# Softmax rounds issued two ahead in a four-layer cross-attention kernel

## What is computed

```python
# layers 0, 3 (latent), H=512, 16 heads of 32
h = jnp.concatenate([x, latents], axis=1)
q = (latents @ q_w + q_b).reshape(b, k_len, NH, DH)
kv = (h @ kv_w + kv_b).reshape(b, p + k_len, NH, DH, 2)
attn = jnp.einsum('bkhd,bnhd->bhkn', q, kmat) / DH
attn = jnp.where(full_mask[:, None, None, :], attn, -jnp.inf)
attn = jax.nn.softmax(attn.astype(jnp.float32), axis=-1).astype(q.dtype)
attn_out = jnp.einsum('bhkn,bnhd->bkhd', attn, v).reshape(b, k_len, H)
attn_out = attn_out @ out_w + out_b + residual
out = rmsnorm(attn_out, postnorm_w)
out = jax.nn.gelu(out @ mlp_w1 + mlp_b1) @ mlp_w2 + mlp_b2
return out + residual
# layer 1 (grouped): 32 query heads on 8 key heads of 16, softmax, Wo, residual, layer norm
# layer 2 (cross): layer norm, q, k, v, 16 heads of 32, softmax, cproj, residual, layer norm, MLP, residual
```

## Time and profile before

| | us |
|---|---|
| median of 3 runs (2697.95 to 2700.19) | 2698.76 |
| the profiled execution | 2698.54 |
| its span | 2696.8 |
| PE busy (92% of the span) | 2478.5 |
| DVE / POOL / ACT busy | 1284.3 / 1104.4 / 1090.2 |

### The profile page before, as it was taken

How to read it: one execution, slowest core, us unless ns; L and a number is a source line. 1 busy time by engine, 2 the same in 40 slices (tenths; PEclk the granted TensorE clock), 3 DMA queues, 4 the chain that set the end, 5 groups by cost and what they waited for, 6 DMA issues and landing times.

```text
span 2696.8 us, 47930 instructions
## 1 busy us (share of the span) xinstructions
PE 2478.5 (92%) x18464; PEld 2080.7 (77%) x18464; DVE 1284.3 (48%) x2527; ACT 1090.2 (40%) x3705; POOL 1104.4 (41%) x1972
## 2 busy tenths in 40 slices
PE   7999998999997777758888899999899999899999
PEld 6887886888886666647777788888788888688887
DVE  4556554323226878764445533322355555432322
ACT  4555553111117777755555411111355555311111
POOL 2444446400135888973454570003345444540000
PEclk9999999999998999879989899999999999899999
DMA  4112213111122222221232241101211211321100
GB/s 154 56 56 89 70 36 106 62 45 47 59 74 70 78 91 77 66 69 61 84 103 89 73 125 48 47 34 61 83 48 48 87 48 34 105 63 47 48 32 16
DMA packets 110321, 181.25 MB, mean 67 GB/s; under 512 B 7889, under 2 KB 43409, under 8 KB 109073
## 3 DMA queue, kind: packets, MB, share of 16 engines
q1 hardware_dynamic: 110096, 178.19, 20.2%
HBM read 132.02 MB, written 46.14 MB: 66 GB/s over the span
## 4 chain that ended last, share of the span: by engine, by line
PE 78%; DVE 8%; ACT 5%; POOL 5%; issue 3%; DMA 1%; SPq 0%; DVEq 0%; POOLq 0%; ACTq 0%
PE banks L317 70%; PE banks L453 4%; ACT plain_high L697 3%; PE banks L480 3%; POOL plain_high L1268 2%; DVE neg_max L948 2%; DVE plain_high L944 2%; PE banks L504 1%; DVE plain_work L953 1%; DVE rounded_work L1046 1%; DVE rounded_work L1020 0%; DVE stats L1072 0%; DMA plain_work<-mlp_w 0%; POOL rounded_high L308 0%; PE banks L442 0%
## 5 line engine op out<-in xcount | busy, mean ns | idle before, releaser
L317 PE MATMUL banks<-rounded_work,rounded_low 128*128 128x512 f32 (+1 forms) x2688 | 533.1, 356 | 57.9 <-issue 35.3
L1268 POOL TENSOR_SCALAR plain_high<-plain_high,inv_sum 128x128 f32<-128x128 f32 (+1 forms) x1024 | 388.1, 402 | 407.7 <-DVE inv_sum L966 407.2
L317 PEld LDWEIGHTS banks<-rounded_work,rounded_low 128*128 128x128 f32 x2688 | 445.7, 200 | 124.7 <-issue 53.8
L317 PE MATMUL banks<-rounded_work,rounded_high 128*128 128x512 f32 (+1 forms) x2400 | 488.2, 358 | 8.7 <-DMA rounded_work<-ctx_split 6.2
L925 ACT ACTIVATE plain_work<-banks,columns 128x512 f32<-128x512 f32 x192 | 132.5, 690 | 865.3 <-PE banks L317 865.3
L317 PEld LDWEIGHTS banks<-rounded_work,rounded_high 128*128 128x128 f32 x2400 | 399.7, 193 | 76.4 <-issue 9.8
L1244 DVE CAST rounded_work<-plain_work 128x512 fp32r<-128x512 f32 x192 | 101.3, 528 | 693.7 <-ACT plain_work L925 682.8
L317 PE MATMUL banks<-rounded_low,rounded_work 128*128 128x512 f32 x1728 | 413.1, 391 | 0.0
L317 PE MATMUL banks<-rounded_high,rounded_work 128*128 128x512 f32 (+1 forms) x1728 | 392.8, 380 | 0.0
L317 PEld LDWEIGHTS banks<-rounded_low,rounded_work 128*128 128x128 f32 x1728 | 322.3, 188 | 68.8 <-issue 3.0
L317 PEld LDWEIGHTS banks<-rounded_high,rounded_work 128*128 128x128 f32 x1728 | 311.8, 190 | 60.4 <-issue 1.4
(11 more groups left out here) (101 smaller groups left out, 3063.4 us busy)
## 6 DMA issues: line engine op xcount, KB each, us to landing
plain_work<-x SPq DMA_DIRECT2D x96, 256.0 KB, 2.9
plain_work<-mlp_w SPq DMA_DIRECT2D x96, 256.0 KB, 2.7
rounded_work<-ctx_split SPq DMA_DIRECT2D x24, 1024.0 KB, 6.0
u<-plain_work SPq DMA_DIRECT2D x48, 256.0 KB, 2.8
plain_work<-u SPq DMA_DIRECT2D x12, 1024.0 KB, 6.7
x<-plain_work SPq DMA_DIRECT2D x48, 256.0 KB, 2.1
plain_work<-attention_w SPq DMA_DIRECT2D x44, 256.0 KB, 2.7
plain_work<-inputs_t SPq DMA_DIRECT2D x8, 1024.0 KB, 8.1
```

What stands on the lines that cost most here:

```text
L317: mm = pe.matmul(dst, lhs(i), rhs(j), start=first and n == 0, stop=last and n == 2, skip_group_check=True)
L1268: last = pool.tensor_scalar(part, part, inv_sum[:, R % 2, r, g:g + 1], 1.0, ALU.mult, ALU.mult)
```

## The change

In every layer a quarter now begins with turning the probabilities of its own round R and then issues the scores of round R + 2; before, it issued the scores of R + 1 first and then turned R. ACT copies both of its turned banks before the exponentials, DVE both of its own before the maxima, and the two inverses of a round are placed one by one, the second behind `dve_heads`. In the cross layer the keys and queries are projected two couples ahead (`pe_cross_pair`), the values one couple ahead, and the first input of the cross layer is turned and split within the last couple of the grouped layer; its DMAs are issued there too. The core of the diff:

```diff
@@ pe_gqa
             for p in range(PAIRS):
                 more = p + 1 < PAIRS
-                pe_scores(pe, y, p, 1)
                 pe_turn_probs(pe, y, p, 0)
+                pe_scores(pe, y, p, 2)
...
-                pe_scores(pe, y, p, 2)
                 pe_turn_probs(pe, y, p, 1)
+                pe_scores(pe, y, p, 3)
...
                 pe_turn_probs(pe, y, p, 3)
+                if more:
+                    pe_scores(pe, y, p + 1, 1)
+                    pe_queries(pe, y, p + 1, 1)
+                pe_attend(pe, y, p, 3)
+                if not more:
+                    pe_turn_x(pe, L[2], 0)
                 pe_out(pe, y, 2 * p)
-                pe_attend(pe, y, p, 3)
@@ pe_cross
+            pe_scores(pe, y, 0, 1)
+            pe_turn_x(pe, y, 1)
+            pe_cross_pair(pe, y, 1)
             for p in range(PAIRS):
...
                 pe_turn_probs(pe, y, p, 0)
                 if more:
-                    pe_turn_x(pe, y, p + 1)
+                    pe_scores(pe, y, p + 1, 0)
+                    pe_values(pe, y, p + 1, 0)
+                if p:
+                    pe_out(pe, y, 2 * p - 1)
                 pe_attend(pe, y, p, 0)
...
+                pe_turn_probs(pe, y, p, 1)
+                if more:
+                    pe_scores(pe, y, p + 1, 1)
+                if far:
+                    pe_turn_x(pe, y, p + 2)
...
                 pe_out(pe, y, 2 * p)
                 pe_attend(pe, y, p, 1)
-                if more:
-                    for i in range(2):
-                        pe_values(pe, y, p + 1, i)
+                if far:
+                    pe_cross_pair(pe, y, p + 2)
@@ act_round
             if turned:
                 act_probs(act, y, *turned, 0)
+                act_probs(act, y, *turned, 2)
             if k is not None:
                 act_exp(act, y, p, k, 0)
-            if turned:
-                act_probs(act, y, *turned, 2)
-            if k is not None:
                 act_exp(act, y, p, k, 1)
             between()
@@ dve_gqa
-                dve_round(dve, y, p, 2, (p, 1), nothing)
+                dve_invert(dve, y, p, 2, 1)
+                dve_round(dve, y, p, 3, (p, 1))
+                dve_invert(dve, y, p, 3, 0)
                 if p:
                     dve_again(dve, y, 2 * p - 1)
                 if more:
                     dve_queries(dve, y, p + 1, 0)
                 dve_heads(dve, y, p, 1)
@@ sp_gqa, last couple
+                else:
+                    wait_filled(sp, v_last(y, p))
+                    sp_c(sp, L[2], 0)
+                    sp_x(sp, L[2], 0)
+                    sp_mask(sp, L[2], 0)
```

346 lines of the change are left out of this document (190 added, 156 removed).

## The result

The changed kernel takes 2735.66 us (median of 4 runs, 2734.2 to 2739.52) against 2698.36 (2692.72 to 2700.19): ratio 1.0146, 95% interval 1.0132 to 1.0159. It is slower by some 37 us, where 12 less were forecast, and outside the range of 2654 to 2718 us. The profiled execution's span is 2737.7 us, 40.9 more than before.

The account below looks back on a forecast made before the run. PE was taken to fill the latent layers and MLPs, a chain across engines to pace the grouped layer. +15 - 20.5 - 3 + 12.5 - 16 = -12 us gave 2686 us; 8-in-10 range 2654 to 2718.

Parts of the forecast that it names:

- The grouped body, +15: Grouped layer, seven couples: a new chain through the ring banks makes a couple 49.6 us against 47.45, +15 us.
- the length of the chain: Grouped layer, each quarter: heads, last turning, scores, first add and maximum, exponentials and ACT's heads take 10.4 us.
- the slower rival: Grouped layer: turning and scores at the lower clock in every quarter, 5.4 us a couple, 38 in all, 2724 us; chance 0.20.
- Layer 0's body, +6 for the inputs and +3 for the ring: Layer 0: keys wait longer for rounded inputs, +6 us; the fourth turning waits for the keys' split, +3 us.
- The step of 8.8 us: Layer 0: from the turning's start to DVE's end of the input rounding, 8.8 us, where turning to keys took 6.99.
- Layer 3's body, +3: Layer 3: the fourth turning waits for the keys' split twice a couple, +3 us; inputs stay hidden behind an output projection.
- The ends, -8 each: Ends of both latent layers: 17.4 us from the MLP's first rows to the MLP instead of 26.1; 8 us taken for each.
- The grouped end, -20.5: End of the grouped layer: 36.4 us instead of 56.9, the 11.10 us wait before the cross layer's first keys gone; -20.5 us.
- The cross layer, -3: Cross layer: -13.5 us from shorter couples, +5 for POOL beside the split, +5.5 for the tail; -3 us.
- the +5 for POOL's contention: Cross layer: DVE's input split meets POOL at work and slows, 0.8 us a couple over six couples, +5 us.
- The rival of 2712 us: Cross layer: each input split waits for a whole POOL instruction, 26 us more than the sum, 2712 us; chance 0.05.
- The chance of 0.25 for slower: Whole kernel: slower by over 0.2%, chance 0.25; the slower rivals were 2724 us (0.20) and 2712 us (0.05).

Follow-up runs that it names:

- e12: The changed kernel with useless identity transposes on PE ahead of the third and fourth turning of each grouped couple; 2738.2 us.
- e13: The changed kernel with the second moments of batch 2p-1 half a quarter later in the grouped layer; 2735.4 us.
- e5: The changed kernel with POOL's root ahead of the norm in the latent layers, and the grouped layer's first norm ahead of wait and memset; 2737.0 us.
- e6: The changed kernel with SP's load of the MLP's first rows issued at the start of the last couple in layers 0, 2 and 3; 2726.8 us.
- e3: The changed kernel with grouped attending directly after the scores and ACT's head copies ahead of the exponentials, DVE likewise; 2723.1 us.
- e11: The changed kernel with the scores ahead of the turning on PE in two of four quarters of a grouped couple; 2733.7 us.

## Why the prediction was wrong

Its sign was wrong because the terms that cost were too small, while those that gain were nearly right: the bodies of the grouped layer and of layers 0 and 3 were put at +27 us together and measured +58.

- **The grouped body, +15, measured +27.2.** The kind was right: DVE's wait for the exponentials went, and the turnings wait for DVE's heads and queries at L453. The idle time of ACT in front of the maximum, 2.3 us a quarter, was 2.9. The step that failed is the length of the chain: "heads on DVE 0.60, last turning 0.65, scores 1.00, first add and maximum 1.43, exponentials 6.15, heads on ACT 0.61: 10.4 us". Where queries stand beside the heads, two turnings wait, and with the low clock they take 1.97 us and the scores 1.49 to 1.67; e12 has 1.17 and 1.00 at the high level. In the quarter of the values the sum would be 10.8 with the 0.3 us of their copies on ACT, and e12's quarter is 10.84 us with fast scores; the change's is 11.51 with scores of 1.67. In the quarter of the residual (ACT's starts 1041.60 and 1054.51) DVE's two copies of turned banks, 1.23 us, stand on the chain, and the sum had none of them. DVE's wait for POOL's root, 1.9 us once a couple, was not in the sum either and is not in the couples of before; but e13 took it away and gave nothing, so by itself it isn't what the sum lacked. Over the seven couples it was 2.15 us a couple more by the forecast and 3.9 by the traces (47.2 to 51.1); 1.74 by seven is the missing 12. How these 1.74 divide the runs don't show.
- **The clock.** The body's sum had 1.2 us a couple for it. In the one couple shown above the turnings and scores of two quarters alone were 2.0 us longer than at the high level (1.97 against 1.17, 1.49 and 1.67 against 1.00). So the slower rival was right in part: its threshold was 51.3 us a couple, and 51.1 was measured; a couple above 51 us was also named as a sign that the forecast is wrong. Its price was too high, though: 5.4 us a couple on top of the sum makes 55.0, and +53 us for the body, where +27.2 was measured. That the total passed its 2724 is due to the latent layers and the ends.
- **Layer 0's body, +6 for the inputs and +3 for the ring, measured +21.4** up to the last couple; it also began 1.7 us later. PE stood 10.1 us longer: 17.4 us of waits for the rounded inputs where 8.8 were, 3.6 for the ring in fourteen waits, and one wait of 2.2 less. The step of 8.8 us from the turning's start to DVE's end was right, 220.52 + 2.36 - 213.92 = 8.96, and so was "0.8 a couple more" in six couples (2.10 against 1.26); in the first it was 4.8 against 1.2. The term that was put at nothing is PE's own time at the lower clock: PE was busy 11.3 us more for the same work, 7.3 of them in those keys. The latent bodies had no term for the clock at all.
- **Layer 3's body, +3, measured +9.3.** The ring cost what was said, 3.5 us in fourteen waits of 0.25; the keys of its second couple waited 2.69 us instead of 0.40 and took 7.33 instead of 5.72. That its inputs "stay hidden behind an output projection" did not hold there.
- **The ends, -8 each.** From the arrival of the first rows to the MLP layers 0 and 3 take 18.2 us, forecast 17.4: right, -8.0 and -9.2. But "the first rows don't come sooner" had to read: they come 4.2 and 4.0 us later. The root of batch 13 stands behind a norm on POOL, and SP's load behind the store of its result. For the cross layer's tail the text counted just this; for the latent layers it did not. e5 and e6 show both halves of it.
- **The grouped end, -20.5, measured -16.8.** Right in kind: no wait ahead of the keys is left. In its place PE waits 4.26 and 4.79 us for the last banks.
- **The cross layer, -3, measured +3.6.** A couple was forecast at 37.9 us; five take 38.3 to 39.5, 4.4 us more together. The couple before them, put at 35.0, takes 39.2. From the last keys to the MLP it is 9.5 us more than before, where 5.5 was said. The waits for the input were 2.1 to 2.9 us where 2.7 was said, and 3.96 at the last; at the turning they were 0.53 where 0.5 was said. Of the +5 for POOL's contention 1.0 was paid, once. The ten casts of the input between 1300 and 1500 us are all fast:

```profile
L1040 DVE CAST rounded_work<-plain_work 128x512 fp32r<-128x512 f32 x10 | 4.3, 428 | 14.1 <-ACT plain_work L764 14.1
```

  POOL stood idle at those splits, since it waited for the next rows (L1319, 6.91 and 7.41 us for a DMA) and began only at their end. But the last cast of the layer met POOL's addition:

```profile
1507.78 0.43 DVE L1040 CAST rounded_work<-plain_work 128x512 fp32r<-128x512 f32 x1 [2.58 <-ACT plain_work L764]
...
1509.18 1.45 DVE L1040 CAST rounded_work<-plain_work 128x512 fp32r<-128x512 f32 x1 [0.24 <-ACT plain_work L764]
...
1509.08 1.26 POOL L1319 TENSOR_TENSOR plain_work<-plain_work 128x512 f32<-128x512 f32 x1 [6.12 <-DMA plain_work<-x]
```

  The keys behind it waited 3.96 us instead of 2.94. The rule of the Trainium skill on the port that GpSimd and VectorE share ("SBUF — State Buffer", SBUF: two separate sides) is that whichever starts first holds it for its whole instruction. This one cast, which ended 0.3 us after POOL's addition, agrees. The rival of 2712 us, in which all four split instructions of six couples would meet POOL, did not come about: in the change the two met at the input's split only here.
- **The start of the grouped layer**, +2.7, was not in the sum. POOL's wait for the stored MLP and its memset stand ahead of the first norm in the changed kernel, where they stood behind it, and the forecast had no term for it. Whether this is the cause was not tested alone: with the norm first and the rest as changed (e5) the stretch takes 5.3 us more.

The chance of 0.25 for slower stood on mechanisms with one price each; that the terms of all three bodies and of the cross layer could be low together, by 37 us, had no case of its own.

## What to carry to other kernels

When a round is started further ahead, the engine that stands idle is decided by what lies between its last instruction of one round and the first input of the next; count every step between them, copies on other engines too, and close the account on that engine (busy plus waits equals the window) before believing a chain. Look for a second and a third chain of nearly the same length before pricing the removal of one: here e3, e11 and e13 each shortened one and the idle time moved elsewhere. Read a filler or any other edit couple by couple before taking its total as an answer: e12's gains and losses hid each other. Place each feeder (the rounding of the next inputs, the turning of the next input, the load of the next rows) by its need and not by its old neighbour; those three edits gave 24, 12 and 9 us, and with the old order of the grouped layer they added up.
